# Moving the weighting of values to the front of an attention unit on TensorE

## The reference, cut to what matters

```
h = h + attn(layernorm(h))
s   = (q @ k.T + q @ r_k[iv, ih]) * scale      # 198 x 198 for each image and head
p   = softmax(s)
out = p @ v + p @ r_v[iv, ih]
y   = out @ proj_w.T + proj_b
```

## Time and profile before

| | us |
|---|---|
| median of 3 runs | 4431.72 (4425.48 to 4433.78) |
| the profiled execution, its own time | 4426.74 |
| its span in the profile | 4425.0 |
| attention stage in it | 514 to 3484 |
| TensorE busy in the span | 4084.1 (92%) |
| VectorE busy | 2922.1 (66%) |
| ScalarE busy | 2506.7 (57%) |
| GpSimd busy | 1273.7 (29%) |

### The profile page before, as it was taken

The page is one execution under the profiler, slowest core; times in us unless marked ns, Lnnn a source line. Parts: engine busy times, 40 slices in busy tenths (PEclk is TensorE's granted clock), DMA queues, the critical chain, the costliest instruction groups (busy, mean ns, idle before and its releaser), DMA issues. The chain is left out here.

```text
span 4425.0 us, 84814 instructions
## 1 busy us (share of the span) xinstructions
PE 4084.1 (92%) x28203; PEld 3987.8 (90%) x28203; DVE 2922.1 (66%) x7468; ACT 2506.7 (57%) x6685; POOL 1273.7 (29%) x1423
## 2 busy tenths in 40 slices
PE   4986799899999999989989999999999799999999
PEld 4885699899899999989989998998999699999999
DVE  4675666666666766666666666666666577777776
ACT  2553666566666666656666666666665344444443
POOL 1232322222232222213222222221322244444443
PEclk8997899999999999999999999999999799999999
DMA  8543000000000000000000000000000222222222
GB/s 184 131 109 73 7 1 1 1 24 1 1 23 1 1 2 23 1 1 23 1 1 19 7 1 2 23 1 1 12 1 1 66 90 89 89 89 89 89 89 87
DMA packets 88973, 161.67 MB, mean 37 GB/s; under 512 B 5705, under 2 KB 75936, under 8 KB 85054
## 3 DMA queue, kind: packets, MB, share of 16 engines
q1 hardware_dynamic: 85118, 152.66, 12.1%
q0 software_dynamic: 944, 2.42, 0.3%
q10 hardware_dynamic: 2576, 2.36, 0.2%
HBM read 127.82 MB, written 29.60 MB: 36 GB/s over the span
## 5 line engine op out<-in xcount | busy, mean ns | idle before, releaser
L631 POOL TENSOR_TENSOR att_prob<-att_prob,att_total 99x396 f32<-99x396 f32 x768 | 650.9, 848 | 2279.0 <-DVE att_total L862 2279.0
L712 ACT ACTIVATE att_probT<-att_t 99x396 f32<-99x396 f32 x768 | 385.0, 501 | 737.4 <-PE att_t L1043 732.0
L870 DVE TENSOR_REDUCE att_npeak<-att_s 99x2 f32<-99x396 f32 x768 | 435.4, 567 | 451.7 <-PE att_s L1077 437.2
L724 ACT ACTIVATE att_prob<-att_s,att_npeak 99x198 f32<-99x198 f32 x1536 | 638.0, 425 | 80.3 <-DVE att_npeak L870 77.5
L1077 PE MATMUL att_s<-att_kx,att_qx 96*99 96x198 f32 (+1 forms) x3072 | 661.9, 339 | 4.5 <-DVE att_xres L841 2.3
L1060 PE MATMUL att_o<-att_probT,att_vx 99*96 99x198 f32 (+1 forms) x3072 | 663.1, 339 | 1.1 <-DVE att_rx L855 1.1
L1257 POOL TENSOR_TENSOR ffn_hidden<-ffn_relu 128x384 f32<-128x384 f32 x462 | 419.7, 914 | 494.8 <-ACT ffn_relu L1286 492.7
L1077 PEld LDWEIGHTS att_s<-att_kx,att_qx 96*99 96x99 f32 (+1 forms) x3072 | 494.3, 170 | 16.3 <-issue 5.3
L1286 ACT ACTIVATE ffn_relu<-ffn_h 128x384 f32<-128x384 f32 x462 | 226.3, 490 | 477.3 <-PE ffn_h L1503 476.5
L1515 PE MATMUL ffn_y<-ffn_down,ffn_hidden 128*128 128x192 f32 x2772 | 487.5, 326 | 0.0
L1060 PEld LDWEIGHTS att_o<-att_probT,att_vx 99*96 99x96 f32 (+1 forms) x3072 | 477.2, 181 | 5.8 <-issue 1.4
(11 more groups left out here) (237 smaller groups left out, 8170.7 us busy)
## 6 DMA issues: line engine op xcount, KB each, us to landing
ffn_gates<-gate_rows SPq DMA_DIRECT2D x66, 768.0 KB, 5.0
tok_pixels<-in_x SPq DMA_DIRECT2D x24, 1568.0 KB
ffn_hid<-hidden SPq DMA_DIRECT2D x35, 288.0 KB, 3.0
att_xres<-hidden SPq DMA_DIRECT2D x8, 1188.0 KB
hidden<-att_xres SPq DMA_DIRECT2D x8, 1188.0 KB
ffn_acc<-hidden SPq DMA_DIRECT2D x33, 288.0 KB, 2.9
out_hidden<-ffn_acc SPq DMA_DIRECT2D x33, 288.0 KB, 2.4
hidden<-tok_rows SPq DMA_DIRECT2D x7, 1176.0 KB
```

Source lines behind the costliest of these rows:

```text
L631: nc.gpsimd.tensor_tensor(prob[:, i % 2, :, :], prob[:, i % 2, :, :], view(total[:, i % 2, :], [[1, 2], [0, NTOK]]), ALU.mult).then_inc(pr ...
L712: nc.scalar.activation(probT[:, i % 2, :], t_bank[0:HALF, 0:2 * NTOK], ACT.Copy).then_inc(probT_made, 1)
L724: ins = nc.scalar.activation(prob[:, i % 2, h, :], s_bank[i % 2][0:HALF, h * NTOK:(h + 1) * NTOK], ACT.Exp, bias=npeak[:, i % 2, h:h + 1], ...
L870: nc.vector.tensor_reduce(npeak[:, i % 2, :], s_bank[i % 2][0:HALF, 0:2 * NTOK].rearrange("p (h k) -> p h k", h=2), AX.X, ALU.max, negate= ...
```

## The change

One call moves. Before, a unit on TensorE ran scores of n, transposes of n - 2, weighting of n - 3, jobs. After, it runs weighting of n - 3, scores of n, transposes of n - 2, jobs. The wait of all readers at a pair's first unit stays ahead of all of them. The steps themselves, their waits, and the programs of the other engines stay as they were.

```
                         if i % UNIT == 0:
                             all_read(base, v, "first", p, max(range(FIRST), key=lambda j: order[v]["first", p, j]))
                         K = 128 if head else 96
+                        if v != "first" or i >= 3:
+                            weigh(n, i, base, v)
                         if v != "first" or i >= 2:
                             pe.wait_ge(exps, n - 1)
                         for h in range(2):
...
                         ins.then_inc(scores, 1)
                         if v != "first" or i >= 2:
                             turn_probs(n, i)
-                        if v != "first" or i >= 3:
-                            weigh(n, i, base, v)
                         for j in spreads[v][i]:
                             job(base, g, v, *j)
```

## The result

The changed kernel takes 4484.65 us (median of 4 runs, 4478.65 to 4490.24) against 4432.75 us before: a ratio of 1.0121, 95% interval 1.0105 to 1.0138, or 52 us. The forecast was 4513 us, 28 us too high; the range of 4458 to 4560 us holds the time, and the forecast's own range (from 4485) just misses it.

A forecast was written before the change was run, and what follows sets the result against it. TensorE was taken to set the pace. The profiled 4426.7 us plus 64 of waits and 18 of clock gave 4508.7; with 5 from profiled execution to median, 4513 us, range 4458 to 4560.

The forecast's parts named there:

- The joints cost nothing: TensorE's step joints: weight loads hide as well behind new neighbours; bounds 0.01 us a unit either way, 8 us in all.
- The loop: Scores, maxima, inverted sums, copy, weighting, next scores: 3.28 us minimum per unit; costs 20 us in short units, 11.5 in last group.
- the fourth rival: Loop longer than forecast, so the more numerous units of 3.36 us pay too: 4586 us, chance 0.12.
- Late copies: Weighting waits for ScalarE's late copy of the transposes, with scores behind it: 1.09 us at each of 16 places, 17 us.
- Borders: At 7 group borders VectorE is behind, so the weighting delays the scores: 1.8 to 1.9 us a border, 13 us.
- The projections at nothing: The 48 projections' waits for VectorE (80.9 us) stay about as they are; otherwise 0.29 us each, 14 us.
- The clock: New and longer TensorE stops bring some 10 more low-clock stretches of 1.7 us each: 18 us, bounds 0 and 68.
- The faster one: VectorE's freed wait shortens the 48 projections' stops (20 us) and the transposes' wait (16.5 us) goes: 4395 us, chance 0.04.
- No change: The order of one engine's steps is free while their sum stays: 4432 us, give or take 8, chance 0.04.
- Only late copies and borders: VectorE reaches its copy sooner, so only late copies, borders and 5 us of clock count: 35 us, 4467, chance 0.17.
- The longer loop: Loop longer than forecast, adding 60 us of waits and some clock: 4586 us, chance 0.12.
- the third rival: Only late copies, borders and some clock cost time, 35 us: 4467 us, chance 0.17.

The follow-up runs named there:

- the run with all places put back: Changed kernel with the old order at units after short ones, late copies, group borders, first and last pair (186 of 768 units): 1.0006 of the kernel before.
- the other job order: Kernel before with the last output table by columns put ahead of the last two query tables and the first projection behind them: 4308.76 us, 0.9722.
- two of its relatives: Changed kernel with an additional VectorE copy per copying out of a weighting: 1.0307; changed kernel with the reordered jobs: 4414.57 us, 0.9968; both against the kernel before.
- the kernel before with the longer copy: Kernel before with one more VectorE copy (64 x 176, PSUM to a spare tile) in each copying out of a weighting: 1.0101, +51 us.
- the kernel with the short units put back: Changed kernel with the weighting behind the transposes again in six units of a group that follow a short unit: 1.0097 of the kernel before.

## Why the prediction was right, and where it was off

**What bounds the kernel.** Right. TensorE is at 92% in both profiles, and 49 of the 56 us stand at the places of the table where its waits or its clock changed; the 7 of "all other units" I can't assign one by one.

**The joints cost nothing.** Right within its bound of 8 us: whole stretches of units differ by 0.08 us or less either way, all other units together by 7.1 us, and the run with all places put back is at 1.0006.

**The loop.** Right, and its size: 3.28 us forecast, 3.31 read. Units of 2.60 us lost 0.71 us each (0.68 forecast) and the last pair 11.4 us (11.5). Units of 3.00 us lost 0.20 instead of 0.28: where VectorE copies out a weighting of 96 rows (99*96 in the timeline) the loop is 3.19 us, so "no unit can be shorter" than 3.28 was 0.1 us too high there. One term was missing. The first pair of the first group has no output tables or projections of a pair before it, so its units are short too; the new waits there are like this one of the profile after:

```profile
536.41 0.88 PE L1060 MATMUL att_o<-att_probT,att_vx 99*96 99x198 f32 x4 [0.94 <-DVE att_rx L855]
```

It cost 8.1 us. I had read short units in one middle group and in the last, and multiplied. The count in the fourth rival has the same hole: 92 units under 3.28 us with 45 us missing, where the trace before has 107 with 57, of which 13 with 11.5 us stand in the first pair.

The row of the weighting's waits for L855 was to show 45 us or more over 90 to 130 times and shows 31.4 us over 55. The units' starts give 37 us for the loop; stops of under 0.2 us are not in the row, and with them the units of 3.00 us.

**Late copies.** Right place, size too large: 0.77 us instead of 1.09. The timeline of the profile after, answering to the earlier trace rows:

```profile
1334.45 0.50 ACT L712 ACTIVATE att_probT<-att_t 99x396 f32<-99x396 f32 x1
...
1335.01 0.94 PE L1060 MATMUL att_o<-att_probT,att_vx 99*128 99x198 f32 x4 [0.91 <-ACT att_probT L712]
```

From the copy's end (1334.95) to the weighting are 0.06 us, where I took the 0.15 of a wait on VectorE; and measured from the scores two units earlier, ScalarE comes 0.51 us sooner than before, not 0.28. That is 0.32 of difference. The second new row has its 33 stops as forecast, but only half of them near 1 us: 16 of 0.9 and 16 of 0.5.

**Borders.** The step "1.8 to 1.9 us a border" was mis-sized: 0.84 us. I let the delay of the maxima reach the long gap. The gap in fact shrank, from 4.44 to 3.9 us, in all 7 places.

**The projections at nothing.** Right: 81.2 against 80.9 us.

**The clock.** This is the term that put the forecast too high: I added 18 us. Between the first and the last scores 119 us ran at the low level against 126, so 3 or 4 us of matmul time were gained, and even that is within the scatter between executions. Next to that the waits were 4 us too high in sum (64 forecast; 56.3 and the 3.5 gained are 60), and the 5 us from profile to median were 2.4.

New stops brought next to no new low stretches. Of the 31 low stretches of the attention stage in the profile after, 15 begin at stops of the projections and 14 at the gaps of a border, just like those before (19 and 14 of 34); one follows a stop of 2.1 us ahead of a weighting, and one stands near the stage's end, as before. The stops that wait for L855 are 0.2 to 1.4 us long, and even the last group's units without jobs, with a stop of 1.3 us in each 3.2, ran like this:

```profile
3462.84 0.91 PE L1060 MATMUL att_o<-att_probT,att_vx 99*128 99x198 f32 x4 [1.26 <-DVE att_rx L855]
3463.59 0.83 PE L1079 MATMUL att_s<-att_kx,att_qx 96*99 96x198 f32 x4
3464.26 0.51 PE L1043 MATMUL att_t<-att_ident,att_prob 99*99 99x99 f32 x4
...
3466.17 0.88 PE L1060 MATMUL att_o<-att_probT,att_vx 99*96 99x198 f32 x4 [1.40 <-DVE att_rx L855]
```

From scores to transposes are 0.67 us, as at full clock. The rule of the Trainium skill ("TensorE: Matmul & The Clock Gate", "HAM oscillation"), by which a wait between bursts makes each next burst start cold, was drawn from longer waits for transfers; it does not show at stops of this length here. Where the projections' stops of 1.5 to 2.3 us went (the other job order), the low time did move, by 60 us.

**The rivals.** The faster one was wrong at its condition: the projections did not end sooner. "No change" was wrong by the loop. "Only late copies and borders" was wrong, as their 18 us are a third of the loss. The longer loop was wrong for this kernel, but right for two of its relatives.

**The sum, and luck.** The mechanism and its size at the short units and in the last pair were worked out and came out. That the waits' sum of 64 us came so near to the 60 is partly luck: the first pair (8) and the rest of the units (5) were missing, and the late copies (4), the borders (7) and the units of 3.00 us (3) were too dear. The lower bound of the range is said to be the middle of the third rival, which is 4467 us and not 4458; the time lies above both.

## What to carry to other kernels

When a step moves ahead in one engine's order, write down the new circle of waits through the other engines and add it up: it is a floor under every round of the loop, and the rounds with the least work pay, the first and the last ones above all. Count these rounds over the whole program, since the first pair was missed by reading one group and multiplying. Include what the other engine has queued ahead of its part, for that stretches the floor. And before reordering around waits of 0.4 us on an engine that isn't the bound, look for the longest wait of the one that is: filling 48 stops with jobs that were ready gave 124 us, where the finest placing of the weighting gave nothing.

## What the runs showed of the hardware that I had not expected

Stops on TensorE did not all count alike for its clock. The change added 56 us of stops that wait for L855 and L712, nearly all of 0.2 to 1.4 us, in place of the transposes' 16.5 us, and no low time that can be told (0.963 to 0.966 in four executions, against 0.960 to 0.966 before). The loss of 48 stops, most of 1.5 to 2.3 us, cut the low time by 60 us, and here all five executions are at 0.969 to 0.971.

It is not the length of the stops alone. In the kernel before with the longer copy the projections' stops grew by 0.3 us on average, and three of four executions have about 0.955, some 76 us more at the low level, the largest single cost of that edit; the fourth, of the same program, has 0.962, and takes 25 us less. And the kernel with the short units put back is at 0.961 to 0.963 with stops of the projections as long as those of the changed kernel. What decides it is not shown by these runs; a difference of 0.005 in the mean clock, some 22 us here, can come with an edit or without one.
